# The last attention turn and the rounded activations of a quantised FFN: order, PSUM banks, and the engine that casts

## The reference

```python
x = x + xattn(layernorm(x), ctx)      # q', k' = relu(features); (q' (k'^T v)) / (q' sum k'); out @ Wo.T + bo
h = layernorm(x)
gate, up = bit_linear(h, w_gate), bit_linear(h, w_up)        # I = 2048
a = subln(up * square(relu(gate))) * subln_weight            # root mean square over the 2048
x = x + bit_linear(a, w_down)
# bit_linear(x, w): x rounded to integers of +-127 by its row's largest magnitude,
#                   w rounded to -1, 0, 1 by its mean magnitude, then the product
```

## Time and profile before

| what | value |
|---|---|
| median of three runs | 426.86 us (424.27 to 429.05) |
| profiled execution, time | 427.15 us |
| its span, first to last instruction | 425.3 us |
| mean granted TensorE clock | 0.976 of full speed |
| PE busy | 387.9 us, 91% |
| DVE busy | 358.9 us, 84% |
| ACT busy | 317.3 us, 75% |
| POOL busy | 222.5 us, 52% |

### The profile page before, as it was taken

The page is one execution under the profiler, slowest core; times in us unless marked ns, Lnnn a source line. Parts: engine busy times, 40 slices in busy tenths (PEclk is TensorE's granted clock), DMA queues, the critical chain, the costliest instruction groups (busy, mean ns, idle before and its releaser), DMA issues.

```text
span 425.3 us, 8214 instructions
## 1 busy us (share of the span) xinstructions
PE 387.9 (91%) x2868; PEld 190.3 (45%) x2886; DVE 358.9 (84%) x723; ACT 317.3 (75%) x446; POOL 222.5 (52%) x207
## 2 busy tenths in 40 slices
PE   3996999999998999999959988999999998999955
PEld 1443545554555554546435433444444443444412
DVE  3758696797899997898958999989999999998972
ACT  4484677798886989968956567787969796979860
POOL 1073729995065935377207837463737455655420
PEclk9996999999998999999969999999999999999989
DMA  7856957851638513967603303333334333334324
GB/s 232 268 162 172 404 193 195 162 142 51 146 114 214 125 51 112 177 122 172 210 29 52 62 15 62 86 89 86 87 81 94 76 87 62 88 87 113 74 50 124
DMA packets 90872, 52.38 MB, mean 123 GB/s; under 512 B 78800, under 2 KB 78800, under 8 KB 90704
## 3 DMA queue, kind: packets, MB, share of 16 engines
q1 hardware_dynamic: 90832, 51.86, 47.9%
HBM read 28.78 MB, written 4.19 MB: 78 GB/s over the span
## 4 chain that ended last, share of the span: by engine, by line
PE 43%; DVE 28%; issue 7%; ACT 6%; POOL 5%; DMA 4%; SPq 4%; DVEq 1%; POOLq 0%; ACTq 0%
PE ps L1326 24%; PE ps L1391 9%; PE ps L1407 6%; DVE amax L1203 4%; DMA ctxl<-o 3%; POOL fl L826 3%; PE ps L1358 2%; DVE w L1198 2%; DVE fl L1054 1%; ACT wst L927 1%; DVE fh L1198 1%; DVE xq L1555 1%; DVE o L1139 1%; PE ps L1374 1%; ACT fh L865 1%
## 5 line engine op out<-in xcount | busy, mean ns | idle before, releaser
L1391 PE MATMUL ps<-tern,area 128*128 128x512 bf16 x496 | 114.1, 383 | 7.2 <-DVE fl L1054 4.2
L1391 PEld LDWEIGHTS ps<-tern,area 128*128 128x128 bf16 x512 | 50.0, 98 | 67.9 <-issue 6.6
L826 POOL TENSOR_TENSOR fl<-fh,w 128x512 f32<-128x512 f32 x32 | 46.3, 1464 | 32.2 <-DVE fh L1198 32.2
L826 POOL TENSOR_TENSOR v<-w 128x512 f32<-128x512 f32 x32 | 40.4, 1275 | 40.1 <-DVE w L1198 40.0
L958 ACT ACTIVATE w<-ps 128x512 f32<-128x512 f32 x64 | 37.3, 582 | 24.1 <-PE ps L1391 24.1
L1326 PE MATMUL ps<-ctxh,w 128*128 128x512 f16 x128 | 42.1, 397 | 6.5 <-DVE ctxl L1042 6.5
L1326 PE MATMUL ps<-xT,w 128*128 128x512 f16 x192 | 45.4, 393 | 0.8 <-DMA xT<-o 0.8
L1326 PE MATMUL ps<-w,oT 128*128 128x512 f16 x192 | 44.0, 379 | 0.0
L1054 DVE SCALAR_TENSOR_TENSOR fl<-ps,fh 128x512 f16<-128x512 f32 x64 | 40.4, 681 | 3.7 <-ACT fh L865 3.5
L962 ACT ACTIVATE qkT<-w 128x512 f32<-128x512 f32 x64 | 40.3, 630 | 2.0
L865 ACT ACTIVATE fh<-ps 128x512 f16<-128x512 f32 x64 | 34.1, 599 | 10.2 <-PE ps L1358 5.6
(11 more groups left out here) (159 smaller groups left out, 876.0 us busy)
## 6 DMA issues: line engine op xcount, KB each, us to landing
tern<-in_wffn SPq DMA_DIRECT2D x24, 512.0 KB, 4.9
out<-o SPq DMA_DIRECT2D x16, 256.0 KB, 2.1
area<-in_ctxT SPq DMA_DIRECT2D x3, 1024.0 KB, 5.7
xs<-in_x SPq DMA_DIRECT2D x3, 1024.0 KB, 9.9
oT<-in_wkT SPq DMA_DIRECT2D x4, 256.0 KB, 5.8
area<-in_ctxT SPq DMA_DIRECT2D x4, 256.0 KB, 6.3
fh<-in_wvT SPq DMA_DIRECT2D x4, 256.0 KB, 6.8
xs<-in_x SPq DMA_DIRECT2D x4, 256.0 KB, 7.7
```

The costliest lines, as they stand in the source:

```text
L826: nc.gpsimd.tensor_tensor(actg[s % 2][:, q], acts[s % 2][:, q], subln[:, q], ALU.mult)\
L1391: mm = nc.tensor.matmul(acc, xqT[:, s % XT, k, :], weights[k][:, 512 * c:512 * c + 512], start=(k == 0), stop=(k == KC - 1))
```

## The change

1. The last turn (`TURNS[3]`) gets another order: O1 stands ahead of the R units, G0 and G1 ahead of all N units, O2 and O3 behind them between G2, G3 and G4, and P0 after G5. `LAST_BANKS` gives R0 to R7 the banks 0 to 7 and moves O2, O3 to 6, 7. The pieces on ACT and DVE are hung behind other units: `ffn` behind Q1, `chunk` 4 behind O1, the second layer norm's pieces between G2 and G11. The statistics of the last group (`STATS2_AT`, `LARGEST2_AT`, `SCALE2_AT`) come one step later; its quantisation stays in steps 10 and 11.
2. `whole` goes from DVE to POOL for tiles 0 to 14. It is a `tensor_copy` that reads every second 16-bit integer (the low halves of the f32 values) and writes bf16. It stands behind `subln_quarter(s, 3)` for tile s - 1, and for tile 14 behind `subln_quarter(15, 2)`. Tile 15 stays on DVE, in halves (`whole_last`).
3. POOL casts the input tiles 0 and 1 ahead of `x_tile(3, 0)`, SP transposes them ahead of `turn_o(2, 2)`; `subln_quarter(0, 0)` and `(0, 1)` stand ahead of the o tiles. The load of the subln weights goes behind one of the reloads.
4. In the last round SP issues the two transposes of tile 15 ahead of the store of tile 13.
5. `down(0)` waits for 15 drained O units and `down(1)` for 16, where `down(0)` waited for 16.

```diff
@@ -41,8 +42,8 @@
 CPM = NCH // 3
 KVW = 2 * HD + 2
 XT = 3
-STATS2_AT = range(2, 8)
-LARGEST2_AT, SCALE2_AT, QUANTISE2_AT, CUBES2_AT = 8, 9, (10, 11), 11
+STATS2_AT = range(3, 9)
+LARGEST2_AT, SCALE2_AT, QUANTISE2_AT, CUBES2_AT = 9, 10, (10, 11), 11
 NB = FF // 512
 PAIRED = 3
 EARLY = 12
@@ -79,13 +80,14 @@
         "V2 V3 W0 "),
     units(
         "F0 F1 O0 F2 F3 F4 F5 F6 F7 Q0 S0 S1 Q1 S2 "
-        "S3 Q2 Q3 R0 R1 R2 R3 O1 R4 R5 R6 R7 G0 N0 "
-        "N1 N2 N3 O2 N4 N5 O3 N6 N7 G1 G2 G3 P0 G4 "
-        "G5 P1 G6 G7 P2 G8 G9 P3 G10 G11 "),
+        "S3 Q2 Q3 O1 R0 R1 R2 R3 R4 R5 R6 R7 G0 G1 "
+        "N0 N1 N2 N3 N4 N5 N6 N7 G2 O2 G3 O3 G4 G5 "
+        "P0 G6 P1 G7 P2 G8 G9 P3 G10 G11 "),
 ]
 
-LAST_BANKS = {"N0": 4, "N1": 5, "N2": 6, "N3": 7, "N4": 4, "N5": 5, "N6": 6, "N7": 7,
-              "O2": 2, "O3": 3, "P0": 6, "P1": 7, "P2": 6, "P3": 7}
+LAST_BANKS = {"R0": 0, "R1": 1, "R2": 2, "R3": 3, "R4": 4, "R5": 5, "R6": 6, "R7": 7,
+              "N0": 4, "N1": 5, "N2": 6, "N3": 7, "N4": 4, "N5": 5, "N6": 6, "N7": 7,
+              "O2": 6, "O3": 7, "P0": 6, "P1": 7, "P2": 6, "P3": 7}
 
 ACT_AFTER = [
     {
@@ -148,11 +150,12 @@
         ("F", 7): (("chunk", 1),),
         ("Q", 0): (("chunk", 2),),
         ("Q", 1): (("chunk", 3),),
-        ("Q", 2): (("kvh",), ("chunk", 4)),
-        ("G", 0): (("chunk", 5),),
-        ("N", 2): (("chunk", 6),),
-        ("N", 6): (("chunk", 7),),
-        ("G", 3): (("root2",),),
+        ("Q", 2): (("kvh",),),
+        ("O", 1): (("chunk", 4),),
+        ("G", 1): (("chunk", 5),),
+        ("N", 3): (("chunk", 6),),
+        ("N", 7): (("chunk", 7),),
+        ("G", 9): (("root2",),),
     },
 ]
 DVE_AFTER = [
@@ -186,13 +189,14 @@
     },
     {
         ("F", 3): (("st2", 0),),
-        ("Q", 2): (("ffn",),),
-        ("N", 4): (("st2", 1),),
-        ("O", 3): (("st2", 2),),
-        ("G", 1): (("st2", 3),),
-        ("G", 2): (("large2",),),
-        ("G", 4): (("scale2",), ("quant2", 0)),
-        ("G", 5): (("quant2", 1), ("cubes2",)),
+        ("Q", 1): (("ffn",),),
+        ("G", 2): (("st2", 1),),
+        ("G", 3): (("st2", 2),),
+        ("G", 5): (("st2", 3),),
+        ("G", 8): (("large2",),),
+        ("G", 9): (("scale2",), ("quant2", 0)),
+        ("G", 10): (("quant2", 1),),
+        ("G", 11): (("cubes2",),),
     },
 ]
 
@@ -627,17 +631,17 @@
             turn_o(2, 0)
             turn_x(3, 3)
             turn_o(2, 1)
-            turn_o(2, 2)
-            turn_o(2, 3)
-
-            sp.wait_ge(filled["K"], G * KC)
-            sp.wait_ge(filled["V"], G * GT)
-            sp.dma_start(subln, sublnw.rearrange("(a n) -> a n", a=1).broadcast_to((P, FF))).then_inc(subln_in, 16)
-            raw_down_again(0)
-            raw_down_again(1)
             for j in range(2):
                 sp.wait_ge(xqb_ok, j + 1)
                 sp.dma_start_transpose(xqT[:, j], xqb[:, j, :]).then_inc(xqT_in[j], 16)
+            turn_o(2, 2)
+            turn_o(2, 3)
+
+            sp.wait_ge(filled["K"], G * KC)
+            sp.wait_ge(filled["V"], G * GT)
+            raw_down_again(0)
+            sp.dma_start(subln, sublnw.rearrange("(a n) -> a n", a=1).broadcast_to((P, FF))).then_inc(subln_in, 16)
+            raw_down_again(1)
             raw_down_again(2)
             raw_down_again(3)
             turn_o(3, 0)
@@ -645,11 +649,13 @@
             turn_o(3, 2)
             turn_o(3, 3)
 
+            def store(t):
+                sp.wait_ge(res_ok, t + 1)
+                sp.dma_start(out_dram[t], res[:, t % 2, :]).then_inc(out_done[t % 2], 16)
+
             for s in range(NT + 3):
-                if s >= 3:
-                    t = s - 3
-                    sp.wait_ge(res_ok, t + 1)
-                    sp.dma_start(out_dram[t], res[:, t % 2, :]).then_inc(out_done[t % 2], 16)
+                if s >= 3 and s != NT:
+                    store(s - 3)
                 j = s + 2
                 if j < NT:
                     sp.wait_ge(xqb_ok, j + 1)
@@ -794,6 +801,10 @@
 
             context_high(3)
             context_low(3)
+            pool.wait_ge(quantised, 1)
+            for j in range(2):
+                pool.wait_ge(ctx_split, G * KC)
+                nc.gpsimd.tensor_copy(xqb[:, j, :], xq[:, j, :]).then_inc(xqb_ok, 1)
             x_tile(3, 0)
             kv_low(2)
             add_bias(2, 0)
@@ -809,6 +820,14 @@
             add_bias(2, 3)
             mask_columns(3)
 
+            def whole(s):
+
+                pool.wait_ge(scaled_ok, s + 1)
+                if s > 1:
+                    pool.wait_ge(aqT_in[s % 2], landed_in(s - 2, 2))
+                low = actg[s % 2].bitcast(I16).rearrange("p (n k) -> p n k", k=2)[:, :, 0]
+                nc.gpsimd.tensor_copy(aq[s % 2], low).then_inc(aq_ok, 1)
+
             def subln_quarter(s, c):
 
                 if c == 0 and s + 2 < NT:
@@ -825,22 +844,21 @@
                 pool.wait_ge(acts_ok, NB * s + c + 1)
                 nc.gpsimd.tensor_tensor(actg[s % 2][:, q], acts[s % 2][:, q], subln[:, q], ALU.mult)\
                     .then_inc(actg_ok, 1)
-
-            pool.wait_ge(quantised, 1)
-            for j in range(2):
-                nc.gpsimd.tensor_copy(xqb[:, j, :], xq[:, j, :]).then_inc(xqb_ok, 1)
+                if c == (3 if s < NT - 1 else 2) and s > 0:
+                    whole(s - 1)
+
             add_bias(3, 0)
             kv_low(3)
+            subln_quarter(0, 0)
+            subln_quarter(0, 1)
             o_tile(3, 0)
             o_tile(3, 1)
-            subln_quarter(0, 0)
             o_tile(3, 2)
             o_tile(3, 3)
-            subln_quarter(0, 1)
+            subln_quarter(0, 2)
             add_bias(3, 1)
-            subln_quarter(0, 2)
+            subln_quarter(0, 3)
             add_bias(3, 2)
-            subln_quarter(0, 3)
             add_bias(3, 3)
             for s in range(1, NT):
                 for c in range(NB):
@@ -1225,14 +1243,13 @@
                 flink(nc.vector.scalar_tensor_tensor(out=dq[:, pair], in0=frstd[:, :], scalar=down_scale[:, 0:1],
                                                     in1=top[:, pair], op0=ALU.mult, op1=ALU.mult))
 
-            def whole(s):
-
-                if s > 1:
-                    dve.wait_ge(aqT_in[s % 2], landed_in(s - 2, 2))
-                width = FF if s < NT - 1 else HALF
-                for h in range(FF // width):
+            def whole_last():
+
+                s = NT - 1
+                dve.wait_ge(aqT_in[s % 2], landed_in(s - 2, 2))
+                for h in range(2):
                     dve.wait_ge(scaled_ok, s + h + 1)
-                    part = slice(width * h, width * h + width)
+                    part = slice(HALF * h, HALF * h + HALF)
                     nc.vector.tensor_scalar(aq[s % 2][:, part], actg[s % 2][:, part], ROUND, None, ALU.subtract)\
                         .then_inc(aq_ok, 1)
 
@@ -1274,15 +1291,13 @@
                     if 1 <= s <= NT:
                         quantiser(s - 1)
                     if s == NT:
-                        whole(s - 1)
+                        whole_last()
                     if s >= 3:
                         result(s - 3)
                     last_group(s)
                 if c == 2:
                     if s in range(2, NT + 1, 2):
                         result_scales(slice(s - 2, s))
-                    if 1 <= s < NT:
-                        whole(s - 1)
                 if c == 3 and s < NT:
                     largest(s, 0)
 
@@ -1400,7 +1415,7 @@
                     pe.wait_ge(res_ok, s - 1)
                 else:
                     pe.wait_ge(signed, NCH)
-                    pe.wait_ge(drained["O"], G * GT)
+                    pe.wait_ge(drained["O"], G * GT - 1 + s)
                 for k in range(FK):
                     if s == NT - 1 and k % (FK // 2) == 0:
                         pe.wait_ge(last_aqT_in[k // (FK // 2)], 16)
```

More of the change, by code:

```diff
@@ L16 @@
 BF16 = mybir.dt.bfloat16
+I16 = mybir.dt.int16
 I16 = mybir.dt.int16
```

5 lines of the change are left out of this document (2 added, 3 removed).

## The result

The changed kernel takes 440.00 us (median of 4 runs, 439.27 to 441.74). The kernel before took 426.88 us beside it. The ratio is 1.0316, with a 95% interval of 1.0250 to 1.0381: slower by 3.2%. The forecast was 434.0, with a range of 424 to 445. The profiled execution has a span of 437.4 us at a mean granted clock of 0.971. Medians are over all runs, ratios compare fast runs alone, and every trace is of a fast run but that of cast_early, which is of its slow one (438.63 us at a granted clock of 0.964; its fast runs took 430.73, 431.37 and 436.73).

The account below looks back on a forecast made before the run. PE and DVE were taken to share the bound, with a two-step FFN loop through the transposed tile. Sum: 425.3 - 1.2 + 8.6 - 1.7 + 1.5 = 432.5 us of span, 434.0 as median; range 424 to 445.

Parts of the forecast that it names:

- start to R: From the start to the end of the last turn's R units, just ahead of G0: about 214.3 us, as before.
- R to a(3): From the R units' end to gate_up(3, 0): G0 starts earlier, without the slow clock; -5.1 us.
- a(3) to a(4): From gate_up(3, 0) to gate_up(4, 0): a 4 us stall at down(1) leaves -1.2 us of the turn's -5.1.
- a(4) to a(14), five pairs: FFN from gate_up(4, 0) to gate_up(14, 0), in pairs of steps: 116.2 us for 107.57, +8.6.
- a(14) to end: From gate_up(14, 0) on: tile 15's transposes go ahead of the store, down(15) starts at down(14)'s end; -1.7 us.
- slow clock: PE's low clock after the 4 us stall at down(1) and a like one at step 10: +1.5 us.
- rival 4: A dear cast on POOL, 4.25 us: 2.35 more in each of five pairs and at down(1), 448; chance 0.13.
- The loop: FFN, over two steps: each us that the transposed tile lands beyond 17.26 after gate_up(s, 0) costs one us.
- L: Time from the start of gate_up(s, 0) to the landing of tile s - 1; at s = 6, 19.6 for 18.16.
- the block on DVE: Step 2: some 14 us of DVE work ahead of multiply(2, 3), so down(1)'s tile lands at 272.9, PE ready at 268.9.
- Rival 3: The last turn's gain is kept (gate_up(4, 0) at 272.5, no slow clock), FFN pays as forecast: 428.7; chance 0.20.
- rival 2: DVE's relief decides: result_scales ends early enough that multiply(s, 3) waits for ACT alone; 422.3 us, chance 0.13.

Follow-up runs that it names:

- cast_early: The changed kernel with the cast behind subln_quarter(s, 2) in every step, not behind (s, 3); 434.05 us, ratio 1.0160.
- cast_norm: The changed kernel, cast kept on GpSimd, with the layer norm's pieces placed as in norm_early; 441.03 us, ratio 1.0346.
- cast_twice: The changed kernel with every cast done twice on GpSimd, one behind the other; 463.07 us, ratio 1.0867.
- spare_cast: turn_only plus the same cast on POOL into memory that nobody reads, with no transpose behind it; 430.56 us, ratio 1.0102.
- norm_early: turn_only with the second layer norm's pieces of the last group one step, or some units, earlier; 421.96 us, ratio 0.9919.
- norm_again: norm_early unchanged, run once more on another chip; 423.62 us, ratio 0.9918.
- turn_only: The changed kernel with whole back on DVE at quarter 2, that is, the change without edit 2; 424.76 us, ratio 0.9981.
- store_first: The changed kernel with edit 4 undone, the store of tile 13 again ahead of tile 15's transposes; 443.64 us, ratio 1.0399.

## Why the prediction was right, and where it was off

The direction, the mechanism and its place were right, and the size was short: the span grew by 12.1 us and not by 7.2. That 440.00 lies well inside the range of 424 to 445 is in part luck: it is the very end of the forecast's own range (429 to 440), and the range went beyond for the sake of a dear cast, which the cast is not. The table sets the prediction's terms against the trace of the changed kernel, all as differences to the trace of before.

| stretch | forecast | measured |
|---|---|---|
| start to R | 0 | -2.7 |
| R to a(3) | -5.1 | -4.5 |
| a(3) to a(4) | +3.9 | +6.4, of it slow down(1) 2.4 |
| a(4) to a(14), five pairs | +8.6 | +14.4, of it slow downs 3.3 |
| a(14) to end | -1.7 | -1.5 |
| slow clock, put in as one term | +1.5 | in the rows above, 5.7 |
| sum | +7.2 | +12.1 |

**The cast: 1.9 us, right.** By groups of the changed kernel (count, busy us, mean ns):

```profile
L829 POOL CAST xn<-v 128x2048 bf16<-128x2048 int16 x8 | 15.1, 1892 | 0.0
...
L829 POOL CAST o<-fl 128x2048 bf16<-128x2048 int16 x7 | 13.2, 1890 | 0.0
```

The casts in a row were the better guide: 1.89 for an estimated 1.9. The Trainium skill's 1.9 cycles per element (GPSIMD Engine Reference, Performance pitfalls for Q7 kernels) would have been 3.2, an estimate; at the page's 1.2 GHz the row shows 1.1 cycles. (The 7 us for this price leave out down(1), which rival 4 counts; with it they are 8.) Rival 4 falls.

**The loop: right, its terms short by 0.3 to 1.2.** Three steps have L = 20.0 for 19.6. The waits came where they were forecast: 2.05, 2.58 and 2.57 us for about 2.3 each, 4.75 for some 4, 16.4 in all for over 12. Of the 0.4 in step 6, result_scales ended at +11.73 instead of +11.4. The stretch from multiply(6, 1) to its end took the 4.57 us that it took before; the 0.3 lie ahead of it. The shorter wait for GpSimd that I had taken off came (0.27 us for 0.52 at 304.53), but DVE then waited 0.35 for ACT's root (305.15). Step 10 was mis-sized most, 22.48 for 21.3. I had counted scale and quantise on DVE, but not that POOL's input cast of tile 12 waits 7.81 us for that quantise, with three sublns queued behind it (the row under cast_norm). POOL and then DVE in step 10:

```profile
358.48 3.72 POOL L845 TENSOR_TENSOR v<-w 128x512 f32<-128x512 f32 x3
...
361.23 0.99 DVE L1578 TENSOR_TENSOR nt<-rstdf 128x2 f32<-128x2 f32 x1
```

An operation of result_scales ends with these sublns and lasts 0.99 us, where it lasts 0.16 in step 6: 0.8 of the 1.2. My own rule, to name what is queued behind a waiting instruction, I applied to the new cast and not to this old one. The five L together are 2.7 us over the forecast.

**The slow clock: the term that was mis-sized most.** I put in 1.5 us for two stalls. My own rows gave more, 1.6 us (3.19 for 1.6) and 1.7 (5.31 for 3.6) behind one stall each. There are three slow downs, 2.41, 1.63 and 1.69, in all 5.7: the two at the foreseen stalls lost 4.1, the third, down(5), was not foreseen; with 2.7 for L it makes 8.4 us, and the rows from a(3) to a(14) miss by 8.3. That it follows a stall was right in kind: the granted clock was 0.68 in down(5) and 1.00 in down(7). How often it does was a guess: of the changed kernel's seven waits for odd tiles, those of 1.62, 2.58 and 4.75 us were followed by a slow down, those of 2.05, 2.57, 1.43 and 1.44 were not. In cast_twice, where most of these waits are longer, six downs were slow, 13.9 us. The cost of being late is therefore more than the lateness.

**The last turn: right to 0.6 us, and lost as forecast.** From R, a(3) comes 4.5 us earlier for 5.1. Then comes the block on DVE: the stall was 2.16 + 1.62 = 3.8 us where I had 4.0, though half of it showed up a unit earlier, at the last quarter of step 3, where an operation of DVE on four elements waits out the cast (1.80 us at 264.79), as in spare_cast. Counted from R, a(4) is 1.9 us later than before. That a(4) looks 0.8 us earlier in the profile is the 2.7 us by which this execution reached R sooner, and those are no part of the change: 2.6 of them are there at the third turn's first R unit (158.44 before, 155.80 after), and from there to R both kernels take 55.9. G0 follows R by 1.5 us for 1.1. norm_early and norm_again, one program, differ at R by 2.7. Rival 3 falls: a(4) is late. turn_only shows that without the cast 2.9 us of the gain are still there at a(4) and are lost by a(10), so at a(4) the loss is the cast's, behind the block on DVE; norm_early shows that the place of the layer norm's pieces holds 3.3 us of what turn_only loses later.

**The end: right.** down(15) follows down(14) at once, and the stretch is 1.54 shorter for 1.7 (2.0 by store_first).

**DVE's relief: rival 2 falls, as argued.** What DVE no longer does became idle time: DVE is idle for 97.4 us of the span where it was for 66.4, 31 us more for the 20 forecast, since the span grew too. DVE's waits from 260 to 400 us in the changed kernel:

```profile
DVE w L1216 <- ACT qkT L980: 20.9, 6, 5.2
DVE fh L1216 <- ACT qkT L980: 5.7, 6, 2.0
```

It waits for ACT, which waits for PE, which waits for the transpose. The loop sets the pace, not DVE's work.

**What it all came from.** From turn_only to the changed kernel a(3) to a(14) grows by 15.2 us. spare_cast puts 4.8 of it on the cast's mere presence on POOL, of which 0.8 is a slow down. The further growth in slow downs is 5.0. The rest, 5.4, is its place in the chain. The prediction had all of it under the place and the clock. The first two depend on the third in the changed kernel (a late landing makes both the waits and the clock), so this split is one way to book it; only the 4.8 was measured alone.

**What stays open.** cast_early still loses 7.2 us against turn_only from a(3) to a(14), 1.7 of it a slow down (in the trace of its longest run), and spare_cast 4.8, so no place on POOL that was tried makes this cast free. A place between subln(s, 3) and the next input cast, or a cast split in halves, was not tried. Why down(7) kept full speed after the same wait as down(5) is not settled. Edits 3 and 5 were not measured alone.
